# Preparing a transformer's quantised weights inside its attention stage, with transposing DMAs, and turning the last stage's quantised activations by DMA

## The reference

```python
x = x + tanh(g_xattn[0]) * mha(layernorm(x), ctx, ctx, W_Q, b_Q, W_K, b_K, W_V, b_V, W_O, b_O)   # 16 heads of 32
x = x + tanh(g_ffn[0]) * bitffn(layernorm(x), w_gate, w_up, w_down)                              # inner size 2048
x = x + tanh(g_xattn[1]) * (softmax(layernorm(x) @ ctx.T) @ ctx)
x = x + tanh(g_ffn[1]) * (mxfp4(layernorm(x), delta_act) @ mxfp4(weight, delta_w).T + bias)

# bitffn: down(silu(gate(x)) * up(x)); each product takes
#   activations round(x * 127 / max|x|), one scale a token, and
#   weights clip(round(w / mean|w|), -1, 1) * mean|w|, one mean for a whole matrix
# mxfp4: blocks of 32 values with a power-of-two scale, values rounded to FP4
```

## Time and profile before

| what | value |
|---|---|
| device time, median of 3 runs | 1709.39 us (1706.91 to 1711.35) |
| device time of the profiled execution | 1708.97 us |
| its span in the profile | 1707.2 us |
| mean granted TensorE clock | 0.939 of full speed |
| busy: PE / DVE / ACT / POOL | 1513.5 / 1233.4 / 873.6 / 905.9 us |
| DMA | 233.90 MB, mean 137 GB/s |

### The profile page before, as it was taken

How to read it: one execution, slowest core, us unless ns; L and a number is a source line. 1 busy time by engine, 2 the same in 40 slices (tenths; PEclk the granted TensorE clock), 3 DMA queues, 4 the chain that set the end, 5 groups by cost and what they waited for, 6 DMA issues and landing times. The chain is left out here.

```text
span 1707.2 us, 25251 instructions
## 1 busy us (share of the span) xinstructions
PE 1513.5 (89%) x7272; PEld 981.8 (58%) x7305; DVE 1233.4 (72%) x2149; ACT 873.6 (51%) x1433; POOL 905.9 (53%) x1162
## 2 busy tenths in 40 slices
PE   4799999998999999998446899999999939999997
PEld 3556666665656666663135455555555417888885
DVE  3567776777767776666374688888888717999985
ACT  3255555555555555554365545555555415555552
POOL 3168566676658566666301433443444115777774
PEclk9899999999999999997667999999999969999998
DMA  5827456473827456470271444444444353445420
GB/s 187 256 63 207 145 159 194 130 216 111 244 79 204 146 157 198 118 204 13 98 272 37 78 107 113 111 110 106 113 111 110 66 185 118 137 148 182 139 68 37
DMA packets 198430, 233.90 MB, mean 137 GB/s; under 512 B 97196, under 2 KB 114104, under 8 KB 194744
## 3 DMA queue, kind: packets, MB, share of 16 engines
q1 hardware_dynamic: 198328, 232.68, 47.3%
HBM read 135.86 MB, written 75.53 MB: 124 GB/s over the span
## 5 line engine op out<-in xcount | busy, mean ns | idle before, releaser
L510 ACT ACTIVATE a_probs<-a_sc 128x512 f32<-128x512 f32 x512 | 300.3, 596 | 298.7 <-PE a_sc L423 296.2
L565 DVE TENSOR_REDUCE a_negmax<-a_mx 128x1 f32<-128x512 f32 x512 | 338.0, 675 | 99.2 <-PE a_mx L406 98.3
L619 POOL TENSOR_TENSOR a_acc<-a_acc,a_probs 128x512 f32<-128x512 f32 x256 | 320.9, 1283 | 6.0 <-ACT a_probs L510 4.4
L619 POOL TENSOR_TENSOR a_acc<-a_probs 128x512 f32<-128x512 f32 x128 | 161.7, 1284 | 243.5 <-ACT a_probs L510 242.6
L406 PE MATMUL a_mx<-a_stack 96*128 96x512 f32 x512 | 227.0, 443 | 32.9 <-DVE a_negmax L565 20.8
L1002 PE MATMUL bank<-w_wgu,b_xq 128*128 128x512 bf16 x1022 | 227.7, 381 | 7.6 <-DMA b_xq<-b_xcode 7.6
L423 PE MATMUL a_sc<-a_stack 97*128 97x512 f32 x512 | 216.2, 424 | 9.5 <-DMA a_stack<-a_mrow 7.5
L571 DVE RECIPROCAL a_attn<-a_den 128x128 f32<-128x128 f32 x128 | 120.8, 948 | 121.5 <-PE a_den L444 121.5
L1002 PEld LDWEIGHTS bank<-w_wgu,b_xq 128*128 128x128 bf16 x1024 | 100.4, 98 | 130.0 <-DMA b_xq<-b_xcode 8.5
L406 PEld LDWEIGHTS a_mx<-a_stack 96*128 96x128 f32 x512 | 100.8, 197 | 102.1 <-DVE a_negmax L565 51.1
L1041 ACT ACTIVATE b_sig<-bank,b_tok 128x512 f32<-128x512 f32 x128 | 87.6, 684 | 92.4 <-PE bank L1002 89.2
(11 more groups left out here) (177 smaller groups left out, 2733.2 us busy)
## 6 DMA issues: line engine op xcount, KB each, us to landing
a_stack<-spill SPq DMA_DIRECT2D x192, 256.0 KB, 4.9
spill<-a_part SPq DMA_DIRECT2D x64, 512.0 KB, 3.4
ctx_t<-a_ct SPq DMA_DIRECT2D x16, 1024.0 KB, 8.5
c_ct<-ctx_t SPq DMA_DIRECT2D x8, 2048.0 KB, 8.1
a_stage<-in_x_dram SPq DMA_DIRECT2D x32, 256.0 KB, 5.0
a_stage<-in_ctx_dram SPq DMA_DIRECT2D x32, 256.0 KB, 2.7
attn_t<-a_attn SPq DMA_DIRECT2D x32, 256.0 KB, 3.0
b_xin<-in_x_dram SPq DMA_DIRECT2D x32, 256.0 KB, 2.7
```

The costliest lines, as they stand in the source:

```text
L510: nc.scalar.activation(probs[:, k, j, :], sc[i % 2][:], ACT.Exp, scale=SCALE).then_inc(exp_done, 1)
L565: nc.vector.tensor_reduce(negmax[:, g % 2, j, t:t + 1], mx[i % 2][:], axis=AX.X, op=ALU.max, negate=True).then_inc(mx_done, 1)
L619: nc.gpsimd.tensor_tensor(acc[:, j], probs[:, 0, j] if k == 1 else acc[:, j], probs[:, k, j], ALU.add)\
```

## The change

- `prepare_weights` is gone; its work is in `attention_phase`. Constants live outside it. The codes get one tensor `wcode` of 12 x 16 x 128 columns, which lies where W_Q, W_K and W_V lie until the last projection; `ct` shares its memory with `wo`, and `bo` with `part`.
- **Sums**: in each of the first 24 groups SP loads half a MB of a weight at tick 20 (`sload`) and ACT takes the magnitudes of 128x1024 at tick 130 (`sum`). In batch 6 of 8 PE adds them over the partitions before its first denominators and DVE makes the means and scales (`wscale`).
- **FP4 weight**: one block in each of batches 1 to 4. DVE has 6 of its 12 steps after the burst of group 0 starts and 6 after that of group 1 (`wquant`); the result is stored to DRAM (`w1_code`).
- **Codes**: in the last batch 13 items (four of gate, four of up, W_O, four of down) of 1 MB each: load, two halves of ACT rounding 30 and 36 ticks later, a DVE clip and a DVE clip in bf16 at +40 and +44, and a transposing DMA at +50 straight into `wcode`. Loads use the memory of `xt` and `wsum`, codes that of `stage`. The products of the FFN read `wcode` with the columns in blocks of 128.
- **Last stage**: `w1_code` and the bias are loaded there, PE turns the weight (16 transposes), ACT and DVE split it, and the first score waits for it. POOL writes the quantised y as bf16 `ycode`, SP turns it with a transposing DMA at 336, ACT copies it to f32r at 470 (`ycopy`), `ffn` moves to 479 and `store` to 502. Turns have four banks and two users. `xload` moves from −190 to −300, `cload` from −400 to −240, `csplit` from −300 to −170, `ctload` from −420 to −250.

```diff
+    wbuf = k0("wbuf", [P, 3, C, 2, D], F32R)
+    wo = k0("wo", [P, C, 2, D], F32R)
+    place["part"] = here()
+    part = k0("part", [P, 2, 2, S], F32R)
+    coef = k0("coef", [P, 3])
+    wcode = nc.alloc_sbuf_tensor_at("wcode", [P, 3 * CH, 16, P], BF16, offset=place["wbuf"])[:]
+    bo = nc.alloc_sbuf_tensor_at("bo", [P, D], F32, offset=place["part"])[:]
...
+        raws = [nc.alloc_sbuf_tensor_at(f"raw{n}", [P, 2048], F32, offset=place["xt"] + 8192 * n)[:] for n in range(2)] + [wsum[:]]
+        codes = nc.alloc_sbuf_tensor_at("codes", [P, 2, 2048], BF16, offset=place["stage"])[:]
...
+        ITEM_AT = [PERIOD * g + tick for g in range(G) for tick in ((4, 40, 76) if g < G - 1 else (4, 40, 76, 112))]
+        QSTEPS = 12
+        CODE_SLOT = [sum(n != WO for n, _ in ITEMS[:k]) % 2 for k in range(len(ITEMS))]
...
+        for g in range(G):
+            base = g * PERIOD
+            ck.add(base + 20, 9, "sload", g)
+            ck.add(base + BURST + 2, 9, "sum", g)
+        ck.add(BURST + at["den"], 9, "wscale")
+        ck.add(-60, 9, "wload1")
+        for n in range(QSTEPS):
+            ck.add(PERIOD * (n // 6) + BURST + n % 6, 9, "wquant", n)
+        ck.add(2 * PERIOD + 30, 9, "wstore1")
+        for k, tick in enumerate(ITEM_AT):
+            ck.add(tick, 9, "rload", k)
+            for h in range(2):
+                ck.add(tick + 30 + 6 * h, 9, "rround", k, h)
+            ck.add(tick + 40, 9, "rclip", k)
+            ck.add(tick + 44, 9, "rcode", k)
+            ck.add(tick + 50, 9, "rturn", k)
+        ck.add(3 * PERIOD + 30, 9, "boload")
+        ck.add(4 * PERIOD - 10, 9, "boscale")
...
+                    elif name == "sload" and b * G + args[0] < 3 * SUMS:
+                        k = b * G + args[0]
+                        n, c = k // SUMS, k % SUMS
+                        if k:
+                            sp.wait_ge(summed, k)
+                        src = wsrc[n][:, c * 2:c * 2 + 2, :] if n != DOWN else wsrc[n][:, c // 2:c // 2 + 1, c % 2 * 1024:(c % 2 + 1) * 1024]
+                        sp.dma_start(wsum[:, 0:1024].rearrange("p (o i) -> p o i", o=src.shape[1]), src).then_inc(s_loaded, 16)
...
+                    elif name == "rload" and b == NB - 1:
+                        k, = args
+                        n, c = ITEMS[k]
+                        if k == 0:
+                            sp.wait_ge(qk_full, 2 * G * NB)
+                        if k == RAWS - 1:
+                            sp.wait_ge(summed, 3 * SUMS)
+                            sp.wait_ge(q_stored, 16 * C)
+                        if k >= RAWS:
+                            sp.wait_ge(r_code, k - RAWS + 1)
...
+                    elif name == "rturn" and b == NB - 1 and ITEMS[args[0]][0] != WO:
+                        k, = args
+                        n, c = ITEMS[k]
+                        sp.wait_ge(r_code, k + 1)
+                        if n == GATE and c == 0:
+                            sp.wait_ge(qk_full, 2 * G * NB)
+                        if n == DOWN and c == 0:
+                            sp.wait_ge(v_full, T * NB)
+                        sp.dma_start_transpose(wcode[:, n * CH + c], codes[:, CODE_SLOT[k], :]).then_inc(r_turned[CODE_SLOT[k]], 16)
...
+                        if it + shift == NB - 2 and g == 0:
+                            pe.wait_ge(summed, 3 * SUMS)
+                            for j in range(J):
+                                last = nc.tensor.matmul(den[DH * j:DH * (j + 1), 256:256 + 3 * SUMS], ones[:], sums[:],
+                                                        start=True, stop=True)
+                            last.then_inc(totalled, 1)
+                            pe.wait_ge(w_step, 1)
...
+                    elif name == "sum" and (it + shift) * G + args[0] < 3 * SUMS:
+                        k = (it + shift) * G + args[0]
+                        act.wait_ge(s_loaded, 16 * (k + 1))
+                        nc.scalar.activation(wsum[:, 0:1024], wsum[:, 0:1024], ACT.Abs, accum_out=sums[:, k:k + 1]).then_inc(summed, 1)
...
+                            half = slice(h * 1024, (h + 1) * 1024)
+                            nc.scalar.activation(raw[:, half], raw[:, half], ACT.Copy, scale=scale_w[:, n:n + 1], bias=ROUND)\
+                                .then_inc(r_round, 1)
...
+                        past = sum(n != WO for n, _ in ITEMS[:k])
+                        dve.wait_ge(r_round, 2 * past + 2)
+                        if past == 0:
+                            dve.wait_ge(t_full, 2 * T * NB)
+                        if past >= 2:
+                            dve.wait_ge(r_turned[CODE_SLOT[k]], 16 * (past // 2))
+                        nc.vector.tensor_scalar(codes[:, CODE_SLOT[k], :], raws[k % RAWS], ROUND, 1.0, ALU.subtract, ALU.min).then_inc(r_clip, 1)
...
+                            nc.vector.tensor_scalar(codes[:, CODE_SLOT[k], :], codes[:, CODE_SLOT[k], :], -1.0, None, ALU.max).then_inc(r_code, 1)
...
-                                last = nc.tensor.matmul(bank[:], xq[:, t % 2, c, :], wgu[:, side, c, m * 512:(m + 1) * 512],
+                                last = nc.tensor.matmul(bank[:], xq[:, t % 2, c, :], gu_code[:, side * M + m, :, c, :],
...
-                            last = nc.tensor.matmul(bank_d[:], hq[:, t % 2, r, :], wd[:, r, :], start=r == 0, stop=r == R - 1)
+                            last = nc.tensor.matmul(bank_d[:], hq[:, t % 2, r, :], wcode[:, 2 * M:3 * M, r, :], start=r == 0, stop=r == R - 1)
...
-        at = dict(cload=-400, cload_step=99, csplit=-300, csplit_step=100, ctload=-420, xload=-190, norm=-70, xturn=-31,
+        at = dict(cload=-240, cload_step=99, csplit=-170, csplit_step=100, ctload=-250, xload=-300, norm=-70, xturn=-31,
                   score=0, recip=58, pturn=74, pv=132, ln2=175, norm2=206, scale=(216, 236, 238, 240), mag=288, quant=(300, 305, 310),
-                  yturn=364, ffn=379, store=402, max=34, exp=44, x3=35, out=23, act_turn=6, act_split=20, pool_split=30,
+                  yturn=336, ycopy=470, ffn=479, store=502, max=34, exp=44, x3=35, out=23, act_turn=6, act_split=20, pool_split=30,
                   dve_turn=13, pool_scale=4, pool_quant=8, pool_ln=0)
...
-        turns = Turns(banks[0:3], [(shift, (name, *args)) for shift, name, args in ck.order()
-                                   if name in ("xturn", "pturn", "yturn")], NB // PAIR, read_out)
+        turns = Turns(banks[0:4], [(shift, (name, *args)) for shift, name, args in ck.order()
+                                   if name in ("xturn", "pturn")], NB // PAIR, read_out)
...
+                    elif name == "yturn":
+                        sync_wait(sp, held, y_done, it, shift, TT, t + 1)
+                        sync_wait(sp, held, yt_done, it, shift, TT, t - 1)
+                        sp.dma_start_transpose(ycodet[:, t % R2], ycode[:, t % R2, :]).then_inc(y_turned[t % R2], 16)
...
+                sp.dma_start(w1raw[:], w1_code).then_inc(w1_loaded, 16)
+                sp.dma_start(bf[:], bias_in.partition_broadcast(P)).then_inc(bf_loaded, 16)
...
+                pe.wait_ge(w1_loaded, 16)
+                for o in range(C):
+                    for c in range(C):
+                        last = nc.tensor.transpose(w1_banks[o][:, c * P:(c + 1) * P], w1raw[:, o, c * P:(c + 1) * P], ident[:])
+                    last.then_inc(w1_turned, 1)
...
+                        if isinstance(it, int) and it + shift == 0 and t == 0:
+                            pe.wait_ge(w1_hi, C)
+                            pe.wait_ge(w1_lo, C)
...
+                    elif name == "ycopy":
+                        wait_count(act, y_turned[t % R2], it, shift, TT // R2, t // R2 + 1, 16)
...
-                        nc.gpsimd.tensor_tensor(blocks(y[:, t % R2, :]), blocks(y[:, t % R2, :]), spread(blk[:, t % R2, 1]),
+                        wait_count(pool, y_turned[t % R2], it, shift, TT // R2, t // R2, 16)
+                        nc.gpsimd.tensor_tensor(blocks(ycode[:, t % R2, :]), blocks(y[:, t % R2, :]), spread(blk[:, t % R2, 1]),
```

More of the change, by code:

```diff
@@ L155, in sem @@
             return ctx.enter_context(nc.semaphore("a_" + name))
[L157 removed]
+        w = {n: wbuf[:, i] for i, n in enumerate("qkv")}
         bias = sb("bias", [P, 3, G], F32)
+        place["xt"] = here()
         xt = sb("xt", [P, C, 2, S], F32R)
[L160 removed]
+        ct = wo
+        place["stage"] = here()
         stage = sb("stage", [P, STAGE, D], F32)
[L162 removed]
+        wsum = sb("wsum", [P, 2 * 1024], F32)
         stack = sb("stack", [P, G, 2, J, S], F32R)
@@ L1375, in split @@
                     return turns.bank(name, t)[:].rearrange("p (c s) -> p c s", c=C)
+                for o in range(C):
+                    act.wait_ge(w1_turned, o + 1)
+                    nc.scalar.activation(w1[:, :, HI, o * P:(o + 1) * P], w1_banks[o][:].rearrange("p (c s) -> p c s", c=C), ACT.Copy)\
+                        .then_inc(w1_hi, 1)
                 def window(it, shift, name, args):
```

442 lines of the change are left out of this document (204 added, 238 removed).

## The result

The changed kernel takes 1737.95 us (median of 4 runs, 1734.97 to 1739.83), the kernel before beside it 1710.37 us (1706.91 to 1711.36): ratio 1.0163, 95% interval 1.0142 to 1.0185. It is 28 us slower. The forecast was 1701.5 us with a range up to 1736: the sign was wrong.

What follows compares the result with a forecast made beforehand. The prediction took PE to set the pace except in preparation, a stage of dependent steps, and the last batch, where slots run at DVE's pace. Terms −85.5 + 4 + 30 + 44 = −7.5 took 1709 to 1701.5 us, range 1656 to 1736.

Steps and rivals of the forecast that it cites:

- six of them at most 3.6 with their waits: Attention before its last batch: six FP4 rounding steps take at most 3.6 us against DVE's idle 3.16; 1 us in all.
- Last batch, +30: Last batch of attention: groups grow by 8, 8, 8 and 6 us from the added items, bounds 12 and 68.
- 3 x 2.5 + 0.5 = 8 each: Groups 1 and 2 of attention's last batch: 2.5 us of DVE an item, plus 0.5, so 8 us each.
- Transposes cost nothing: Last batch of attention: a 128x2048 transpose lands after 4.3 us, an item has over 5, no engine waits: 0 us.
- Last phase, +44: Last phase: sum of five terms, −12 + 44 + 12 − 2 + 2 = +44 us.
- (b): Last phase: each batch's first value product waits for the later fourth context split, seven times 5.8 us and once 3.7: +44 us.
- (c): Last phase: after idle PE the clock is 0.50 for 2.8 us of work, losing 1.4; for eight times +12 us.
- (a): Last phase: one PE turn of three goes, 0.43 us over 28 tiles: −12 us.
- (d): Start of the last phase: token rows load first, but 1 MB of rounded weights comes before them: −2 us.
- (e): Tail of the last phase: a transposing DMA landing after 2.4 us, plus issue, replaces a PE turn of 1.11: +2 us.
- the value product does not wait: Rival, last phase: something else in its tile is later anyway, so no wait or slow clock: 1645.5 us, chance 0.10.
- Slower, by a lock: Rival, last batch: DVE passes wait out POOL's additions, then hold POOL; batch grows by 68 us: 1739.5 us, chance 0.21.

## Why the prediction was wrong, step by step

- **Preparation removed, -85.5:** right, to 0.1 us.
- **Attention before its last batch, +4:** +9.3, inside 0 to 20. The sums and small loads in the start-up were no dearer than taken: the first denominator comes at 97.1 us, before at 98.0; the term that failed is "six of them at most 3.6 with their waits". Six steps took 6.0 us (314.61 to 320.6, one other of 0.68 among them) because two met POOL's additions, and the reciprocal came 1.9 us later. Three a burst brought half of the growth back.
- **Last batch, +30:** +40.1 with its end, inside 12 to 68. DVE's item was sized almost right: 2.67 us for 2.5, its bf16 pass bare 0.65 for 0.6, its wait 0.7 in this pass and 0.1 in the clip, for 0.35 twice. The step that failed is that ACT's part lies beside DVE's in groups 1 and 2 ("3 x 2.5 + 0.5 = 8 each"). They grew by 10.2 and 11.3, and cutting ACT's roundings took 7.2 us off these two and 9.7 off the batch. Maximum, score and exponential form one ring through DVE, PE and ACT with two banks each, and as I read it new work in order on any of them counts; that rests on the cuts, which nearly add up (9.7 and 12.3 alone, 18.1 together). The third item's load behind the first transpose, taken at 4 in group 0, was 8.2 with the engines cut (33.7 to 25.5).
- **Transposes cost nothing:** right for their landing, wrong for the queue that issues them, which the prediction priced in group 0 alone. They stood 1.5 to 5.5 us each on SyncE where a plain copy of the same bytes took 0.5, and loads queued behind them: 6 us in the batch. That is far from the 251 us which the 1309 ns a block of the Trainium skill (VectorE: DVE Perf Modes, "The three transpose paths") would give as an estimate. The twelve of the last batch landed 4.3 us after their issue in the median: as before, the rows speak against taking it block by block.
- **FFN, 0:** right; 457.7 against 458.7 us. The matmuls for gate and up, and for down, have means of 381 and 386 ns, before 381 and 387: four runs of 128 columns as moving operand cost nothing.
- **Last phase, +44:** +66.8. The mechanism of (b) and (c) was right in place, releaser and count, and the run of the old kernel with late ticks shows that it stands alone. The sizes were not. (a) -12: with the splits early the stretch is 11.6 us shorter than before, 9 of it by the turn. (b) 5.8 a batch was 7.2. The step that failed is that (b) is read from one tile of the old kernel with PE's time and POOL's time left as they were, while (a) takes the turn of y off that same PE. With the old tile 5.8 was good: the old kernel with late ticks has 5.7 in the mean. In the changed kernel PE is free 1.2 us earlier against POOL, and that is added to the gap; 0.43 of it is the turn, as an estimate from the old row. The rest fits POOL's loop, which the run with the splits one tile earlier shows at 9.2 us, around a tile that PE could do in 8.4: POOL falls behind within a batch, as the intervals of 9.1 to 9.4 us before the long ones show. There the split in its new place pushes the layer-norm steps back in every tile, and they feed the scaling that the fourth split waits behind. So POOL's bias addition, which (b) has end 4.2 us after PE is free ("1 us earlier when its old split ... has gone"), ends 5.7 us after it in the changed kernel, and 4.45 in the old one with late ticks. The first batch's wait was 3.55 for 3.7. (c) 1.4 was 2.6: the whole value product ran at half clock, not its first 2.8 us. (d) and (e), -2 and +2, were -0.3 and +0.1.

The intervals add up: against 8.4 us a tile, the eight long ones carry 73 us and the five of 9.1 to 9.4 us 4, and 258 + 77 = 335 us of the 336.9.

The -7.5 of the sum was the difference of large terms. Ten us missed in the last batch, five in the body and 23 in the last phase turned it. Of the rivals, "the value product does not wait" is excluded. "Slower, by a lock" came within 2 us of the measured time by luck, not by its reason: DVE does wait for POOL, about 10 us in twelve items (0.7 + 0.1 us each), but the last batch grew by 40 us and not by 68, and the last phase brought the rest of the loss.

## What to carry to other kernels

- When a change takes work off one engine, read every wait again in which that engine is the one that waits: it now comes earlier. A gap of 5.7 us became 7.2.
- A step moved later in a schedule has two prices: the deadline of who reads its result, and what now stands behind it in its own queue. Work out both, for each engine that it visits; here they were 58 and 20 us, and one line of ticks gave back 78.
- In this ring of engines with two buffers, work added on two engines nearly added up (9.7 and 12.3 us alone, 18.1 together), though each looked half idle in the windows. Idle shares say what may fit, the order of the queue says what does.
- Large items in a queue of small urgent ones should be issued early and spread evenly. Here spreading gave 7 us in the last batch, while loads issued early handed part of the wait on to the next small transfer.
